# Constant matrix products in seven waits of a graph and expert kernel

## What is computed

```
x = x + gcn(layernorm(x))           # counts of edges (625x625) times (x @ W)
x = x + ffn0(layernorm(x))          # 12-head self attention, then a layer of
                                    # 8 experts (top 2) and one shared expert
x = x + gat(layernorm(x))           # attention over the edges, 12 heads of 64
x = x + ffn1(layernorm(x))          # 8 experts (top 2), hidden width 1536
```

## Time and profile before

| | |
|---|---|
| runs | 1588.89, 1594.05 and 1585.57 us, median 1588.89 |
| the profiled execution's own time | 1588.82 us |
| its span, first to last instruction | 1587.0 us |
| mean granted clock of TensorE | 0.959 |
| PE, DVE, ACT, POOL busy | 92%, 79%, 56%, 20% of the span |

### The profile page before, as it was taken

The page is one execution under the profiler, slowest core; times in us unless marked ns, Lnnn a source line. Parts: engine busy times, 40 slices in busy tenths (PEclk is TensorE's granted clock), DMA queues, the critical chain, the costliest instruction groups (busy, mean ns, idle before and its releaser), DMA issues.

```text
span 1587.0 us, 36908 instructions
## 1 busy us (share of the span) xinstructions
PE 1463.7 (92%) x14608; PEld 1267.9 (80%) x14608; DVE 1252.8 (79%) x2183; ACT 885.6 (56%) x1290; POOL 324.0 (20%) x252
## 2 busy tenths in 40 slices
PE   7999788878999999999998889857999999999997
PEld 5777566656678999999996744447899999999995
DVE  8999777765566888888888589867988887888785
ACT  4214377765345666777773245554566666666651
POOL 1000146650300000000013067734700000000050
PEclk9999999998999999999999689969999999999999
DMA  7550000005656888898873011028788888888884
GB/s 202 151 131 8 11 1 2 1 2 181 199 175 227 281 283 303 289 311 301 297 271 97 10 32 34 25 90 297 263 306 299 293 292 295 294 292 301 286 266 104
DMA packets 55555, 297.60 MB, mean 188 GB/s; under 512 B 14063, under 2 KB 14319, under 8 KB 32433
## 3 DMA queue, kind: packets, MB, share of 16 engines
q1 hardware_dynamic: 41761, 263.23, 48.9%
q0 software_dynamic: 13712, 33.26, 7.8%
HBM read 264.07 MB, written 32.34 MB: 187 GB/s over the span
## 4 chain that ended last, share of the span: by engine, by line
PE 69%; DVE 18%; ACT 3%; POOL 3%; issue 3%; DMA 2%; SPq 0%; POOLq 0%; DVEq 0%; ACTq 0%
PE ps L766 14%; PE ps L745 9%; PE ps L747 9%; PE ps L749 9%; PE ps L2380 5%; PE ps L2363 5%; DVE wl L1462 3%; DVE wl L1463 3%; DMA ext<-in_units 2%; POOL wl L1016 2%; PE ps L2492 2%; PE ps L2292 2%; PE ps L2178 2%; DVE wl L622 2%; PE ps L778 1%
## 5 line engine op out<-in xcount | busy, mean ns | idle before, releaser
L745 PE MATMUL ps<-big,wh 128*128 128x176 f16 x2160 | 495.6, 239 | 8.9 <-DVE wl L622 6.7
L749 PE MATMUL ps<-big,wl 128*128 128x176 f16 x2160 | 495.6, 238 | 0.0
L747 PE MATMUL ps<-big,wh 128*128 128x176 f16 x2160 | 495.6, 238 | 0.0
L766 PE MATMUL ps<-big,wh 128*128 128x176 f16 x2160 | 264.0, 239 | 4.8 <-DVE big L656 4.8
L766 PE MATMUL ps<-big,wl 128*128 128x176 f16 x1080 | 249.6, 240 | 0.0
L622 DVE SCALAR_TENSOR_TENSOR wl<-ext,wh 128x2304 f16<-128x2304 f32 x90 | 229.6, 2551 | 1.5 <-issue 1.2
L622 DVE SCALAR_TENSOR_TENSOR wl<-raw,wh 128x2304 f16<-128x2304 f32 x90 | 229.4, 2549 | 0.0
L541 ACT ACTIVATE wh<-raw 128x2304 f16<-128x2304 f32 x90 | 190.4, 2117 | 60.3 <-PE ps L766 51.4
L745 PEld LDWEIGHTS ps<-big,wh 128*128 128x128 f16 x2160 | 208.4, 97 | 13.2 <-DVE wl L622 6.7
L541 ACT ACTIVATE wh<-ext 128x2304 f16<-128x2304 f32 x90 | 190.5, 2117 | 50.4 <-PE ps L766 32.6
L747 PEld LDWEIGHTS ps<-big,wh 128*128 128x128 f16 x2160 | 210.9, 98 | 0.2
(11 more groups left out here) (376 smaller groups left out, 2794.5 us busy)
## 6 DMA issues: line engine op xcount, KB each, us to landing
raw<-in_units SPq DMA_DIRECT2D x54, 1152.0 KB
ext<-in_units SPq DMA_DIRECT2D x54, 1152.0 KB
raw<-in_units SPq DMA_DIRECT2D x36, 1153.0 KB, 6.2
ext<-in_units SPq DMA_DIRECT2D x36, 1153.0 KB, 7.7
raw<-in_units_s SPq DMA_DIRECT2D x16, 769.0 KB, 4.4
ext<-in_units_s SPq DMA_DIRECT2D x16, 769.0 KB, 4.5
x_slots<-logs SPq DMA_DIRECT2D x1, 8976.0 KB
big<-x_slots POOLq DMA_DIRECT2D x17, 528.0 KB, 8.4
```

What stands on the lines that cost most here:

```text
L745: nc.tensor.matmul(o, wh[:, u % RING, w_], x_, start=c == 0 and m == 0, stop=False, skip_group_check=True)
L747: nc.tensor.matmul(o, wh[:, u % RING, w_], xTl[:, c, 0:ph.n], start=False, stop=False, skip_group_check=True)
L749: ins = nc.tensor.matmul(o, wl[:, u % RING, w_], x_, start=False, stop=c == KC - 1, skip_group_check=True)
L766: ins = nc.tensor.matmul(o, l_[:, u % RING, w_], r_, start=first and k == 0 and c % 2 == 0, stop=last and k == 2, skip_group_check=True)
```

## The change

A helper `kept_busy(b, n)` issues n products on PE: the identity as weights (125 by 128), 512 columns of column numbers moving, into all of bank b, each by itself (start and stop). Nothing reads these results. There are no new waits and no new semaphores. It is called at seven places: 21 products before the transpose of tile 4 in the first half of `sides_transposed(0)`, 25 ahead of the fence, 7 ahead of the wait for `s_fold` 4, 6 ahead of `z_transposed(0)`, 35 behind the last `head_back`, 18 ahead of `ranks(1)` and 23 behind it. That is 135 products. Nothing is removed or moved.

```diff
--- before.py
+++ after.py
@@ -2229,12 +2229,19 @@
                         ins.then_inc(s_agg, 1)
             counts_turned(NT - 1)
 
+            def kept_busy(b, n):
+
+                for _ in range(n):
+                    nc.tensor.matmul(bank(b), ident16[0:P, :], iota16[0:P, 0:BANK], start=True, stop=True)
+
             def sides_transposed(h):
 
                 for s in range(2):
                     if h:
                         pe.wait_ge(s_wTv, 2 * (h * NT - 3) + s - 1)
                     for t in range(NT):
+                        if h == 0 and s == 0 and t == NT - 1:
+                            kept_busy(7, 21)
                         if h == 0:
                             pe.wait_ge(s_vl, t + 1)
                             pe.wait_ge(s_vh, 2 * t + 2)
@@ -2316,6 +2323,7 @@
                 if 1 <= h <= H:
                     for k in ((), (), (0,), (1, 2), (3, 4))[t]:
                         weighted_chunk(h - 1, k)
+            kept_busy(3, 25)
             fence(pe, F_MHA)
 
             def rows_turned(layer, of, t):
@@ -2409,6 +2417,7 @@
             nc.tensor.transpose(bank(6)[:, 0:128], wpair[:, 0, :], ident[:, :])
             nc.tensor.transpose(bank(6)[:, 160:160 + KC], wrow[:, :], ident[0:KC, 0:KC])
             nc.tensor.transpose(bank(6)[:, 128:128 + 2 * H], attn, ident[0:2 * H, 0:2 * H]).then_inc(s_fold, 1)
+            kept_busy(5, 7)
             pe.wait_ge(s_fold, 4)
             nc.tensor.matmul(bank(7)[:, 0:2 * H], wpairT, attnT, start=True, stop=True).then_inc(s_fold, 1)
 
@@ -2444,6 +2453,7 @@
                                            wpair[:, 1, :], start=True, stop=True)
                 ins.then_inc(s_res, 1)
 
+            kept_busy(5, 6)
             z_transposed(0)
             z_transposed(1)
             pe.wait_ge(s_fold, 6)
@@ -2532,13 +2542,16 @@
                     head_chunk(h, t)
             head_chunk(H - 1, 4)
             head_back(H - 1)
+            kept_busy(3, 35)
             for t in range(3):
                 rows_turned(1, z, t)
             for t in range(NT):
                 logits(1, t)
                 if t + 3 < NT:
                     rows_turned(1, z, t + 3)
+            kept_busy(6, 18)
             ranks(1)
+            kept_busy(6, 23)
             rows_transposed, up, down, out_transposed = e1 = tensor_steps(pe, ph_1)
             pe.wait_ge(s_place, 1)
             pe.wait_ge(s_rest, NT)
```

## The result

| | before | changed |
|---|---|---|
| median of the runs | 1587.99 us (18 runs, 1580.29 to 1594.05) | 1596.54 us (18 runs, 1587.18 to 1602.40) |
| the profiled execution's own time | 1588.82 us | 1587.18 us |
| its span | 1587.0 us | 1585.5 us |
| mean granted clock | 0.959 | 0.976 |

The ratio is 1.0053, with an interval of 1.0038 to 1.0068: 8.4 us slower, where 8.0 was forecast. I compare stretches between fixed milestones instead.

A forecast was written before the change was run, and what follows sets the result against it. The matrix engine (PE), busy 92% of the span and 69% of the chain, was taken as the bound. Terms 4.7 + 3.6 - 1.2 + 0.9 = 8.0 us on 1588.82 gave a forecast of 1596.8 us, range 1588 to 1603.

The forecast's parts named there:

- First fill: Behind tile 3, ahead of tile 4's transpose: 21 products, starting at half clock, delay ScalarE's copy by 4.7 us; range 2.3 to 7.8.
- Second fill: Ahead of the fence: 25 products make PE last there, so engines behind it start 3.6 us later; range 0.6 to 5.3.
- Weighing the rule on the spacing: Skill's 131 ns per 512-column product would make the sum 4.7 instead of 8.0 us; the trace's 0.22 us was preferred.
- Third and fourth: Waits before the fold product and following transposes: 7 and 6 products cost 0, keep the clock up, gain 1.2 us.
- Fifth and sixth: Around the logits: fifth fits its wait and saves 0.4 us; sixth starts at half clock, 1.6 late, ranks save 0.3; together +0.9.
- Seventh: Behind the ranks: 23 products, 5.0 us, fit a 5.50 us wait at full clock; VectorE's table sets the chain: 0.
- the clock holds: Rival: full clock lasts over the pauses behind fills one, two and four; -0.9 us, 1587.9, not slower; chance 0.14.
- The products do not hold the clock: Rival: all added products run at 0.43 us from where the clock falls today; 24 us slower, 1613; chance 0.05.
- The fifth stretch goes the other way: Rival: shifts let 888 to 909 us start warm, about 6 us gained, 1590.8, chance 0.14; reverse cold stretch 1601, chance 0.12.

The follow-up runs named there:

- the second of before: The kernel before, unaltered, run and profiled a second time: 1587.50 us, ratio 0.9983.
- the doubled fill: The kernel with only the second fill, given 25 more products (50 ahead of the fence): 1599.93 us, ratio 1.0073 to the kernel before.
- the kernel with the eight alone: The kernel before with no fills, but 5 and 3 products in two short PE waits before the 888 to 909 us stretch: 1583.37 us, ratio 0.9973.
- the moved fills: Changed kernel with the first fill one tile earlier and the second split, 8 products ahead of the fence and 18 behind: 1585.92 us, ratio 0.9972 to before.
- the changed kernel again: The changed kernel, unaltered, run for a second profile: 1599.76 us against 1587.90 for the kernel before, ratio 1.0074.

## Why the forecast was right

The sum of the steps, 8.0 us, stands beside 8.4 measured, and the stretches at the places give nearly the same without the medians: side, fence, the way from the fence to L1221, fold, logits and ranks come to +6.9, +8.2 and +10.0 us in the three profiles of the changed kernel against the first of before, a mean of 8.4. Against the second of before they are +8.1, +9.4 and +11.2, a mean of 9.6. The path was as forecast; that the number is so close is partly luck, for four terms missed by 0.5 to 1.0 us and nearly cancel: by their means the first was 0.7 too large, the second 1.0 too small, the gain of the third and fourth 0.6 too large, the loss of the fifth and sixth 0.5 too large. Step by step:

- *First fill, 4.7.* Measured 3.6, 4.3 and 4.0 in three profiles, 3.7 alone. The mechanism was as put: behind tile 3, started at half clock, ScalarE late by what sticks out, half clock again behind it (0.54 over 202 to 209), no repayment. The term was some 0.7 too large. The fills took 6.04, 6.74 and 6.41 us, for 6.7 forecast; in the first the rise came 2.7 us after the start, less than my nearer bound of 2.9, in the second after 4.1, near the 4.3 that I took. Moved ahead of tile 3 it cost nothing.
- *Second fill, 3.6.* Measured 5.2, 3.5 and 5.2, and 3.5 alone. In the profiles with 3.5 all 25 products ran at the full clock; in those with 5.2 the clock fell within half a microsecond of the fill's start, and 7 or 8 products ran at half; a fall during the fill I had only as a bound (1.7 more), and it came true in two of three. In those two it went to half again within the pause behind; in the second profile it held over the pause and fell at 369.2, half a microsecond into the transposes, which gave back 0.5 us. So in two of three profiles of the whole change the term was 1.6 too small.
- *Weighing the rule on the spacing.* 25 products in 5.56 us and 50 in 10.96 give 0.22 us each. The Trainium skill (TensorE: Matmul & The Clock Gate, "Back-to-back issue gap") states about 131 ns sustained at 512 columns; an estimate from that figure is that the doubled fill would have added 3.3 us, and not the 5.4 that it did. The trace disagrees with that figure, and the measurement decides.
- *Third and fourth, -1.2.* "fold" is 17.6 in each kernel that has them and 17.6 to 18.8 in those that have not (18.2 in the first profile of before). Cost nothing: right. The gain was mis-sized, 0.6 rather than 1.2, because the transposes, 1.3 us faster, give it back in the wait for ScalarE (2.78 for 1.51). Against the second profile of before it is 1.2, and the kernel with the eight alone has 17.6 without these fills; so how much of it is theirs is not shown.
- *Fifth and sixth, +0.9.* "logits" is 1.9, 0.3 and 0.3 shorter, forecast 0.4. The 1.9 is not the fill's own: before has it too, in its second profile, and with fill 1 alone "logits" is 0.9 shorter. "ranks" is 0.6, 1.7 and 1.7 longer, forecast 1.6 less 0.3. In the second and third profile the sixth fill started at half clock as said (6.87 and 6.89 us for the 6.0 forecast), after the clock had fallen among the transposes and logits, as I had expected from the earlier trace rows. In the first it started at the full clock, which fell 0.8 us later (5.73). The loss is gone where the fill is left out. The fifth was priced at the full clock throughout; in the first profile 7 of its 35 products ran at half, and it ended at 1051.96, so that the transposes behind it started some 0.6 us later than DVE's rows allowed (an estimate: in the second profile they start 0.73 us after L2096 does, here 1.31).
- *Seventh, 0.* 9.9 us from the ranks to the table in every kernel, with the fill and without.

Of the rivals, *the clock holds* fell: after each of the first two fills it was back at half within the next pause or half a microsecond behind it, and even where the moved fills held it to 197 and 364, the gain was nothing and 0.7 us. *The products do not hold the clock* fell too: each first fill ended at the full clock, and the second ran wholly at it in one profile of three. (Its term for the second place, 6.6, comes out 0.3 larger when 16 products at 0.43 follow 9 at 0.22.) *The fifth stretch goes the other way* came true in the first and third profiles of the changed kernel (21.4 and 21.2 for 28.4, so 7 us for the 6 that I had put without a row for it), but not in the second (27.2), and 1.7 to 5.7 us of it went again in the heads loop. I had it as a case apart; it is rather a scatter that lies under every case. Outside the places the three profiles differ from the first of before by -8.4, +4.5 and -1.9 us. That the forecast met the median so closely owes something to this scatter's coming out near zero.

What stays open: the parts do not add. By their ratios fill 1 alone costs 4.1 us, fill 2 alone 1.0 and the other five bring 5.2, about 0 together, for 8.4 of all seven. The intervals (some 3.6, 2.7 and 2.8 us either way, and 2.4 for the whole) leave little room for chance. At the places themselves the parts come to 6.7 (3.7, 3.5, -0.5), against 6.9, 8.2 and 10.0 for the whole: two of the three have the fall at the second fill (1.7), and two a "ranks" longer by 0.9 than with the other five alone. So most of the difference lies elsewhere, probably in the stretches without fills. Which of their values a kernel takes, and why the full set takes the longer heads loop (134.4 in three of four profiles that have all seven in place, 128.7 to 131.8 in those with a part or with two moved, but 133.9 too in one of before), no run here settles: each kernel has one to three profiles, not a distribution.

## What to carry to other kernels

A fill belongs ahead of the wait that it is to cover, and ahead of a fence it has only the time until the other engines arrive; price it at half clock where it starts after a pause. Then look at what follows: a faster stretch is worth something only where PE, and not a copy on another engine behind it, sets the end. Here eight products of 2 us together, in two short waits just ahead of a stretch of nearly all PE work, brought 4.3 us, while 135 in longer waits cost 8.4.

## What the runs showed of the hardware that I had not expected

- The stretch behind the fold and the heads loop take only a few values, to a tenth of a microsecond, in different kernels: 28.4, 27.0 to 27.2, 26.0, 24.4, 21.2 to 21.4 and 19.9 us for the one; 128.7, 130.1 to 130.4, 131.8 and 133.9 to 134.5 for the other. What differs with them is where the granted clock falls (0.51, 0.60, 0.92 and 1.00 over the stretch in profiles with 28.4, 26.0, 21.4 and 19.9). This may be a good part of the 14 us between the extreme runs of an unaltered kernel; no profile was taken of those.
- A fall can catch a dense run: at the fence 25 products without a gap had half clock for 3.0 and 3.4 us in two profiles of three, though PE had worked just before (the fall came 0.4 us before the fill, over the last sums, and 0.2 us after its start); the transposes behind them ran wholly or for the most part at half clock in all. In the four profiles in which the 25 or 50 ran whole, the clock had fallen and come back some microseconds before (352.1 to 355.5 in the changed kernel again, fill at 358.8); in the two in which it fell, it had not. That is seen side by side and not tested.
- Holding the clock is not what pays. The changed kernel has the higher mean clock (0.976, 0.970 and 0.971 for 0.959) and is slower.
